# A GNN block kernel on one core: its opening in another order

## The chip, the cores and the metric

One NeuronCore of a Trainium2 chip. The metric is device time in microseconds, the median of several executions. The engines are TensorE (PE), VectorE (DVE), ScalarE (ACT) and GpSimd (POOL); SyncE (SP) only issues DMAs here. All engines run their own instruction streams and meet through semaphores.

## The reference, cut to what matters

Four residual layers on x of 384 x 1024, each of the form x = x + layer(relu(layernorm(x))). Only the first one's start is touched:

```python
h = jnp.maximum(_layernorm(x, axis=-1), 0.0)
q = h @ wq.T + bq
k = h @ wk.T + bk
v = h @ wv.T + bv
q2 = (q @ wiq.T + biq) ...
mask = full((N, N), -inf); mask[src, dst] = softplus(edge_type_weights)[edge_type_5 - 1]
scores = einsum(q2, k2) * scale + mask
```

Then come an output projection, a relational GNN layer (8 relations, counts of edges by type edge_type_8), a SAGE layer and a sparse linear layer, all on the same 6144 edges.

## The kernel before, in words

x lies as three row tiles of 128 x 1024 (NT = 3), a matrix of 1024 x 1024 as eight column tiles (KT = 8). Every fp32 operand is split into a high part of type fp32r and a low part (value minus high part), and a product is three matmuls, high x high, high x low, low x high. For the first five projections PE works through column tiles: `column_tile` (L464 to L477) is 24 matmuls of 128 x 384, eight blocks k times three. Column tile j writes PSUM bank j % 2, so `eight_tiles` (L500) has PE wait before each tile until the tile two before it has been evacuated (the semaphore out_lo): ACT writes the high part (L1005), DVE the low part (L1400).

The order of everything is written out by hand, engine by engine, and nothing reorders it. The opening, which is what the change touches, runs like this.

- **SP** (L278 to L280) issues the three row tiles of x, then from L332 the weights: each column tile of wq comes in four pieces of 128 KB into one of four raw buffers. Ahead of the fifth tile it waits for the edge rows, stores them to DRAM (L341), waits for that store and reads them back broadcast (L285).
- **ACT** issues the four edge lists and the edge type weights (L903, L906). Then per row tile: `norm_std` (L910) takes the root of the variance, `norm_relu_0` (L930 to L934) writes relu(x * rstd + shift) to h0, tiles 0 and 1 in one instruction and tile 2 in two halves (`START`). `start_high` (L937 to L942) evacuates the transposed tile from PSUM as the high part of acts. `tile_high` (L946 to L955) rounds a transposed weight tile to its high part. After the second weight tile come two activations with table loads (L993, L995) for the softplus, and the copy of the transposed biases (L998).
- **DVE** takes the statistics of each row tile (L1262, L1266), `norm_shift` (L1273 to L1277) the reciprocal and the shift, then edge keys (L1289 to L1295), three small operations on the type weights (L1298 to L1300), `turn_tile(0, 0)` (L1329 to L1333, a transpose of the first weight tile in 32 x 32 blocks), the four `start_low` (L1351 to L1357, the low parts of acts, each behind its `start_high`), with the copy of the transposed edges between the first and the second, and `turn_tile(0, 1)`. Then low part of tile 1, `turn_tile(0, 2)`, the softplus remainder behind ACT's logarithm, three mask blocks, and the loop of L1393, whose first pass turns tile 3, makes the low part of tile 2, takes two edge comparisons (`meet`, L1302 to L1316) and only then evacuates column tile 0.
- **PE** transposes each normalised row tile (L488), with the edge rows (L426) between tiles 1 and 2, then the biases (L493), which wait for six small DMAs issued by POOL, and then begins the column tiles. The first one waits at k = 0 until three `start_low` are done, at k = 4 until all four (`turned_at`).
- **POOL** makes constants, issues the six bias DMAs (L1789), makes the low part of the first weight tile (L1794), and then, behind the copy of the edges, three subtractions (L1799).

## Time and profile before

| | |
|---|---|
| median of 3 runs | 928.07 us (927.96 to 932.13) |
| the profiled execution | 927.87 us, its span 926.1 us |
| PE busy | 906.8 us, 98% of the span |
| DVE, POOL, ACT busy | 611.5, 492.3, 359.2 us |
| data moved | 128.60 MB, mean 139 GB/s |

The span is the time from the first instruction to the last one as the profiler has it; the execution around it is 1.8 us longer. A row of a timeline gives start, duration, engine, line, operation, output <- inputs. In brackets is the idle time of the engine before it and what ended it. Line numbers are those of the kernel before.

### The profile page before, as it was taken

Reading aid. Unit: us, or ns where it says so; the run is one execution under the profiler, and the core shown is the slowest. Engines: PE = TensorE matmul, PEld = TensorE weight load, DVE = VectorE, ACT = ScalarE, POOL = GpSimd, SP = SyncE. Lnnn points to the kernel's source line nnn. Section 1 sums busy time; section 2 is a strip of 40 time slices with the busy share of each in tenths; the row PEclk is TensorE's granted clock in tenths of the full one; section 3 lists DMA queues with packets and bytes.
Section 4 is the critical chain, followed back from the end, with each engine's and each line's share of the span. In section 5 each row is a group of like instructions: output and inputs, shape, how many; then the busy total and the mean of one; then the engine's idle time right before and its main releaser. Section 6 shows DMA issues by size and latency. Waiting matters only on the chain.

```text
span 926.1 us, 13755 instructions
## 1 busy us (share of the span) xinstructions
PE 906.8 (98%) x4787; PEld 799.0 (86%) x4787; DVE 611.5 (66%) x993; ACT 359.2 (39%) x558; POOL 492.3 (53%) x436
## 2 busy tenths in 40 slices
PE   4999999999999999999999999999999999999998
PEld 4999999998888888888888888888888878888886
DVE  6998888896996735665656565565656565434545
ACT  6433333345885343223223223232325235224422
POOL 5334446775765515757657575756686402220463
PEclk8999999999999999999999999999999999999999
DMA  8998756634336644344554444444333534323412
GB/s 207 241 277 224 229 155 151 167 85 119 53 52 204 178 155 146 92 151 114 152 152 130 153 113 150 113 148 111 97 91 137 182 98 154 114 93 91 140 42 91
DMA packets 89907, 128.60 MB, mean 139 GB/s; under 512 B 34480, under 2 KB 67456, under 8 KB 89856
## 3 DMA queue, kind: packets, MB, share of 16 engines
q1 hardware_dynamic: 72784, 123.54, 43.8%
q0 software_dynamic: 15552, 0.11, 4.0%
q10 hardware_dynamic: 1520, 4.30, 1.4%
q8 instruction: 29, 0.48, 0.2%
q14 instruction: 22, 0.18, 0.1%
HBM read 117.17 MB, written 7.59 MB: 135 GB/s over the span
## 4 chain that ended last, share of the span: by engine, by line
PE 90%; DVE 3%; ACT 2%; POOL 1%; DMA 1%; issue 1%; POOLq 0%; DVEq 0%; ACTq 0%
PE ps L682 49%; PE ps L476 17%; PE ps L756 9%; PE ps L520 4%; PE ps L645 4%; PE ps L600 2%; PE ps L543 2%; PE ps L556 2%; DMA weight_d<-weight_sum,cell 1%; PE ps L435 1%; POOL weight_d L1890 1%; PE ps L892 1%; DVE wlo_all L1388 1%; POOL mean_lo L1869 0%; PE ps L443 0%
## 5 line engine op out<-in xcount | busy, mean ns | idle before, releaser
L1388 DVE TENSOR_TENSOR wlo_all<-raw,whi_all 128x1024 fp32r<-128x1024 f32 x120 | 200.4, 1681 | 119.6 <-ACT whi_all L972 118.5
L476 PE MATMUL ps<-acts,whi_all 128*128 128x384 f32 (+1 forms) x640 | 164.1, 337 | 0.8 <-DVE acts L1400 0.6
L1869 POOL TENSOR_TENSOR mean_lo<-mean_f,mean_hi 128x384 fp32r<-128x384 f32 x76 | 88.3, 1162 | 120.4 <-ACT mean_hi L1124 120.4
L1124 ACT ACTIVATE mean_hi<-mean_f 128x384 fp32r<-128x384 f32 x76 | 39.9, 525 | 277.2 <-DVE mean_f L1562 277.2
L682 PE MATMUL ps<-whi_all,mean_hi 128*128 128x512 f32 x452 | 139.5, 390 | 0.3 <-POOL mean_lo L1869 0.3
L682 PE MATMUL ps<-wlo_all,mean_hi 128*128 128x512 f32 x452 | 139.3, 389 | 0.0
L682 PE MATMUL ps<-whi_all,mean_lo 128*128 128x512 f32 x452 | 139.3, 389 | 0.0
L972 ACT ACTIVATE whi_all<-raw 128x1024 fp32r<-128x1024 f32 x120 | 125.1, 1050 | 32.0 <-PE ps L682 28.5
L476 PEld LDWEIGHTS ps<-acts,whi_all 128*128 128x128 f32 x640 | 116.8, 190 | 1.2 <-DVE acts L1400 0.9
L1890 POOL DMA_INDIRECT weight_d<-weight_sum,cell x48 | 95.5, 1989 | 30.4 <-DMA weight_d<-weight_sum,cell 17.5
L476 PE MATMUL ps<-acts,wlo_all 128*128 128x384 f32 (+1 forms) x320 | 107.6, 336 | 0.0
L1833 POOL DMA_INDIRECT count_d<-met,cell x48 | 81.3, 1693 | 45.2 <-DMA count_d<-met,cell 32.0
L682 PEld LDWEIGHTS ps<-whi_all,mean_lo 128*128 128x128 f32 x452 | 84.9, 188 | 17.7
L682 PEld LDWEIGHTS ps<-wlo_all,mean_hi 128*128 128x128 f32 x452 | 84.9, 188 | 17.6
L682 PEld LDWEIGHTS ps<-whi_all,mean_hi 128*128 128x128 f32 x452 | 83.8, 188 | 12.6 <-issue 0.7
L1820 POOL DMA_INDIRECT mask_d<-type_val,cell x48 | 52.8, 1100 | 68.1 <-DMA mask_d<-type_val,cell 58.1
L1562 DVE TENSOR_TENSOR mean_f<-ps,inv 128x384 f32<-128x384 f32 x76 | 42.1, 554 | 60.5 <-PE ps L756 59.1
L1864 POOL TENSOR_TENSOR h_row_lo<-h,h_row_hi 128x1024 fp32r<-128x1024 f32 x9 | 24.6, 2756 | 99.1 <-ACT h_row_hi L1119 99.1
L756 PE MATMUL ps<-rel_r,h_row_lo 128*128 128x384 f32 x192 | 64.9, 338 | 0.0
L756 PE MATMUL ps<-rel_r,h_row_hi 128*128 128x384 f32 x192 | 64.9, 338 | 0.0
L1005 ACT ACTIVATE acts<-ps,bcol 128x384 f32 x40 | 23.3, 582 | 100.7 <-PE ps L476 87.9
L682 PE MATMUL ps<-whi_all,h_t_hi 128*128 128x512 f32 x192 | 60.8, 398 | 0.6 <-DVE wlo_all L1388 0.5
(211 smaller groups left out, 1705.6 us busy)
## 6 DMA issues: line engine op xcount, KB each, us to landing
raw<-in_L_gnn_weight SPq DMA_DIRECT2D x64, 512.0 KB
rows_b<-rows_d SPq DMA_DIRECT2D x24, 384.0 KB, 4.8
raw<-in_L_gnn_w_gate SPq DMA_DIRECT2D x16, 512.0 KB
raw<-in_L_gnn_W_self SPq DMA_DIRECT2D x16, 512.0 KB
raw<-in_L_gnn_W_neigh SPq DMA_DIRECT2D x16, 512.0 KB
count_d<-total_r SPq DMA_DIRECT2D x8, 576.0 KB
rel_r<-count_d SPq DMA_DIRECT2D x8, 576.0 KB, 4.5
raw<-in_L_gnn_wq SPq DMA_DIRECT2D x32, 128.0 KB
```

Source lines behind the costliest of these rows:

```text
L476: mm = pe.matmul(ps[:, j % 2, 0:N], stationary[j % RING][:, k, :], acts[:, a, moving, k, :], start=i == 0, stop=i == 3 * KT - 1)
L520: mm = pe.matmul(ps[:, V_BANK[n % 4], 0:V_COLS].rearrange("p (j o) -> p j o", j=2), acts[:, 3, a, k, P * nt:P * nt + P], weight[:, slots, ...
L682: mm = pe.matmul(ps[:, 2 * nt + f, :], stationary[a][:, k, P * nt:P * nt + P], weight[slot][:, HALF * f:HALF * f + HALF], start=first and ...
L756: mm = pe.matmul(ps[:, 7 - k % 2, 0:N], h_row[a][:, s, P * k:P * k + P], edges[:, s, :], start=i == 0, stop=i == 2 * NT - 1)
L972: act.activation(whi_row[slot], raw[slot][:, :], ACT.Copy).then_inc(S["w_hi"], 1)
L1124: act.activation(mean_of(q, k, 0)[:, 0, :], sums_of(q, k), ACT.Copy).then_inc(S["mean_hi"], 1)
L1388: dve.tensor_tensor(wlo_row[slot], raw[slot][:, :], whi_row[slot].bitcast(F32), ALU.subtract)\
L1562: dve.tensor_tensor(sums_of(q, k), ps[:, 7 - k % 2, 0:N], inv[:, :], ALU.mult)\
L1820: pool.indirect_dma_start(mask_d, bass.IndirectOffsetOnAxis(ap=cell[:, 0, c:c + 1], axis=0), type_val[:, c:c + 1], None).then_inc(mask_sca ...
L1833: pool.indirect_dma_start(count_d, bass.IndirectOffsetOnAxis(ap=cell[:, 1, c:c + 1], axis=0), met[:, 1, c:c + 1], None, compute_op=ALU.add)\
L1869: pool.tensor_tensor(mean_of(q, k, 1)[:, 0, :], sums_of(q, k), mean_of(q, k, 0)[:, 0, :].bitcast(F32), ALU.subtract).then_inc(S["mean_lo"], 1)
L1890: pool.indirect_dma_start(weight_d, bass.IndirectOffsetOnAxis(ap=cell[:, 2, c:c + 1], axis=0), weight_sum[:, c:c + 1], None, compute_op=AL ...
```

## The change

It reorders the opening. The first row tile of x comes in two DMAs of half its columns, and DVE takes the statistics of each half as it lands. `norm_shift` of a tile now stands between the two halves of the next tile's statistics. Row tile 2 is normalised by DVE (`start_norm`, without the relu) rather than by ACT, and the relu is applied when ACT and DVE evacuate the transposed tile. The keys of the edges are made early, types and relation keys (`edge_types`) behind the normalisation of tile 2. PE turns the edge rows behind all three tiles, into PSUM bank 2, and the biases behind the first column tile. DVE copies the turned edges and does the three small operations on the type weights behind the fourth `start_low`, just ahead of `turn_tile(0, 1)`.

```diff
--- before.py
+++ after.py
@@ -164,7 +164,7 @@
         ps = ctx.enter_context(nc.psum_tensor("ps", [P, 8, 512], F32))
 
 
-        names = """x_in edges_in etw_in bcol_in brow_in out_stored
+        names = """x_in ends_in edges_in etw_in bcol_in brow_in out_stored
             rows_stored mask_based tables_zeroed weights_zeroed mask_in weight_in
             ident_made order_made spare_made zeros_made ones_made mask_base_made
             key_made edge_rows edges_turned edge_cols edges_moved met_made rows_free
@@ -189,6 +189,7 @@
         weights_added = [sem(f"weights_added{q}") for q in range(GROUP)]
         rel_in = [sem(f"rel_in{i}") for i in range(2)]
         x_part = [sem(f"x_part{nt}") for nt in range(NT)]
+        x_half = sem("x_half")
         v_staged = [sem(f"v_staged_{s}") for s in ("even", "odd")]
 
 
@@ -276,7 +277,9 @@
         @block.sync
         def _(sp_):
             x_rows = x.rearrange("(t p) d -> p t d", p=P)
-            for nt in range(NT):
+            sp_.dma_start(xres[:, 0, 0:HALF], x_rows[:, 0, 0:HALF]).then_inc(x_half, 16)
+            sp_.dma_start(xres[:, 0, HALF:D], x_rows[:, 0, HALF:D]).then_inc(x_part[0], 16)
+            for nt in range(1, NT):
                 sp_.dma_start(xres[:, nt, :], x_rows[:, nt, :]).then_inc(x_part[nt], 16)
 
             def key_rows(s):
@@ -423,7 +426,7 @@
             def turn_edges():
                 pe.wait_ge(S["edge_rows"], 1)
                 for f in range(4):
-                    mm = pe.transpose(ps[:, 0, EC * f:EC * f + EC], e_row[:, f, :], ident[0:EC, 0:EC])
+                    mm = pe.transpose(ps[:, 2, P + EC * f:P + EC * f + EC], e_row[:, f, :], ident[0:EC, 0:EC])
                 mm.then_inc(S["edges_turned"], 1)
 
             def turn_two(y, source, f):
@@ -481,17 +484,18 @@
 
             pe.wait_ge(S["ident_made"], 2)
             for n, (nt, k0, k1) in enumerate(START):
-                if n == 2:
-                    turn_edges()
                 pe.wait_ge(S["h_ready"], n + 1)
                 for k in range(k0, k1):
                     mm = pe.transpose(ps[:, 2 + 2 * nt + k // 4, P * (k % 4):P * (k % 4) + P],
                                       h0[:, nt, P * k:P * k + P], ident[:, :])
                 mm.then_inc(S["start_turned"], 1)
-            pe.wait_ge(S["bcol_in"], 16 * 6)
             pe.wait_ge(S["start_lo"], 1)
-            pe.transpose(ps[:, 2, 0:6 * KT], b_in[:, :], ident[0:6 * KT, 0:6 * KT]).then_inc(S["bcol_made"], 1)
-            pe.wait_ge(S["edge_cols"], 1)
+            turn_edges()
+
+            def turn_biases():
+                pe.wait_ge(S["bcol_in"], 16 * 6)
+                pe.wait_ge(S["edge_cols"], 1)
+                pe.transpose(ps[:, 2, 0:6 * KT], b_in[:, :], ident[0:6 * KT, 0:6 * KT]).then_inc(S["bcol_made"], 1)
 
             def turned_at(k):
 
@@ -567,7 +571,10 @@
                 turn_probs(0, 0)
                 turn_probs(0, 1)
 
-            eight_tiles(0, 0, ready=turned_at)
+            pe.wait_ge(S["out_lo"], O_CREDIT - 1)
+            column_tile(0, 0, 0, turned_at)
+            turn_biases()
+            eight_tiles(0, 0, first=1)
             with pe.Fori(1, 3) as g:
                 eight_tiles(g, 0)
             with pe.Fori(3, 5) as g:
@@ -900,7 +907,8 @@
         @block.scalar
         def _(act):
             for f, field in enumerate((src, dst, et8, et5)):
-                act.dma_start(e_in[:, f, :], field.rearrange("(c p) -> c p", p=P)).then_inc(S["edges_in"], 16)
+                act.dma_start(e_in[:, f, :], field.rearrange("(c p) -> c p", p=P))\
+                   .then_inc(S["ends_in" if f < 2 else "edges_in"], 16)
             act.wait_ge(S["ones_made"], 1)
             act.activation(std[:, 0, :], epsc[:, :], ACT.Sqrt).then_inc(S["ones_made"], 1)
             act.dma_start(etw_b[:, :], etw.partition_broadcast(P)).then_inc(S["etw_in"], 16)
@@ -938,8 +946,8 @@
 
                 nt, k0, k1 = START[n]
                 act.wait_ge(S["start_turned"], n + 1)
-                act.activation(acts[:, 0, 0, k0:k1, P * nt:P * nt + P], start_block(nt, k0, k1), ACT.Copy)\
-                   .then_inc(S["start_hi"], 1)
+                act.activation(acts[:, 0, 0, k0:k1, P * nt:P * nt + P], start_block(nt, k0, k1),
+                               ACT.Copy if nt < NT - 1 else ACT.Relu).then_inc(S["start_hi"], 1)
 
             HALVES = [slice(0, HALF), slice(HALF, D)]
 
@@ -980,10 +988,8 @@
             norm_relu_0(*START[0])
             norm_std(0, 1)
             norm_relu_0(*START[1])
+            norm_std(0, 2)
             start_high(0)
-            norm_std(0, 2)
-            norm_relu_0(*START[2])
-            norm_relu_0(*START[3])
             tile_high(0, 0)
             start_high(1)
             start_high(2)
@@ -1276,28 +1282,44 @@
                 dve.tensor_scalar(shift[:, nt, :], mv[:, nt, 0:1], rstd[:, nt, :], -1.0, ALU.mult, ALU.mult)\
                    .then_inc(S["shift_ready"], 1)
 
-            def start_stats(nt):
-
-                dve.wait_ge(x_part[nt], 16)
-                norm_stats(0, nt)
-
-            for nt in range(NT):
-                start_stats(nt)
-                if nt < NT - 1:
-                    norm_shift(0, nt)
-            dve.wait_ge(S["edges_in"], 16 * 4)
-            dve.scalar_tensor_tensor(e_row[:, KEY, :], e_in[:, 0, :], float(N), e_in[:, 1, :], ALU.mult, ALU.add)\
-               .then_inc(S["key_made"], 1)
-            dve.scalar_tensor_tensor(e_row[:, KEY_T, :], e_in[:, 1, :], float(N), e_in[:, 0, :], ALU.mult, ALU.add)
-            norm_shift(0, NT - 1)
-            dve.tensor_copy(e_row[:, TYPE, :], e_in[:, 3, :])
-            dve.wait_ge(S["key_made"], 1)
-            dve.scalar_tensor_tensor(e_row[:, REL_KEY, :], e_in[:, 2, :], float(N * N), e_row[:, KEY, :],
-                                     ALU.mult, ALU.add).then_inc(S["edge_rows"], 1)
-            dve.wait_ge(S["etw_in"], 16)
-            link(dve.tensor_scalar(sp[:, 0, :], etw_b[:, :], 0.0, None, ALU.max))
-            link(dve.tensor_scalar(sp[:, 1, :], etw_b[:, :], -1.0, None, ALU.mult))
-            dve.tensor_tensor(sp[:, 2, :], etw_b[:, :], sp[:, 1, :], ALU.max).then_inc(S["sp_max"], 1)
+            def edge_keys():
+
+                dve.wait_ge(S["ends_in"], 16 * 2)
+                dve.scalar_tensor_tensor(e_row[:, KEY, :], e_in[:, 0, :], float(N), e_in[:, 1, :], ALU.mult, ALU.add)\
+                   .then_inc(S["key_made"], 1)
+                dve.scalar_tensor_tensor(e_row[:, KEY_T, :], e_in[:, 1, :], float(N), e_in[:, 0, :], ALU.mult, ALU.add)
+
+            def edge_types():
+
+                dve.wait_ge(S["edges_in"], 16 * 2)
+                dve.tensor_copy(e_row[:, TYPE, :], e_in[:, 3, :])
+                dve.wait_ge(S["key_made"], 1)
+                dve.scalar_tensor_tensor(e_row[:, REL_KEY, :], e_in[:, 2, :], float(N * N), e_row[:, KEY, :],
+                                         ALU.mult, ALU.add).then_inc(S["edge_rows"], 1)
+
+            def start_norm(nt, k0, k1):
+
+                dve.wait_ge(S["shift_ready"], nt + 1)
+                dve.tensor_scalar(h0[:, nt, :].rearrange("p (f b i) -> p b f i", f=KT, b=4)[:, :, k0:k1],
+                                  xres[:, nt, :].rearrange("p (b f i) -> p b f i", f=KT, b=4)[:, :, k0:k1],
+                                  rstd[:, nt, :], shift[:, nt, :], ALU.mult, ALU.add).then_inc(S["h_ready"], 1)
+
+            dve.wait_ge(x_half, 16)
+            half_stats(0, 0)
+            dve.wait_ge(x_part[0], 16)
+            half_stats(0, 1)
+            var_of(0, 0)
+            edge_keys()
+            dve.wait_ge(x_part[1], 16)
+            half_stats(1, 0)
+            norm_shift(0, 0)
+            half_stats(1, 1)
+            var_of(0, 1)
+            dve.wait_ge(x_part[2], 16)
+            half_stats(2, 0)
+            norm_shift(0, 1)
+            half_stats(2, 1)
+            var_of(0, 2)
 
             def meet(n):
 
@@ -1352,19 +1374,31 @@
 
                 nt, k0, k1 = START[n]
                 dve.wait_ge(S["start_hi"], n + 1)
-                dve.tensor_tensor(acts[:, 0, 1, k0:k1, P * nt:P * nt + P], start_block(nt, k0, k1),
-                                  acts[:, 0, 0, k0:k1, P * nt:P * nt + P].bitcast(F32), ALU.subtract)\
-                   .then_inc(S["start_lo"], 1)
+                low, high = [acts[:, 0, a, k0:k1, P * nt:P * nt + P] for a in (1, 0)]
+                if nt < NT - 1:
+                    dve.tensor_tensor(low, start_block(nt, k0, k1), high.bitcast(F32), ALU.subtract)\
+                       .then_inc(S["start_lo"], 1)
+                else:
+                    dve.scalar_tensor_tensor(low, start_block(nt, k0, k1), 0.0, high.bitcast(F32), ALU.max,
+                                             ALU.subtract).then_inc(S["start_lo"], 1)
 
             dve.wait_ge(S["h_ready"], 1)
             turn_tile(0, 0)
+            norm_shift(0, 2)
+            start_norm(*START[2])
+            start_norm(*START[3])
+            edge_types()
             start_low(0)
-            dve.wait_ge(S["edges_turned"], 1)
-            dve.tensor_copy(e_col[:, :, :], ps[:, 0, 0:4 * EC].rearrange("p (f c) -> p f c", f=4))\
-               .then_inc(S["edge_cols"], 1)
             start_low(1)
             start_low(2)
             start_low(3)
+            dve.wait_ge(S["edges_turned"], 1)
+            dve.tensor_copy(e_col[:, :, :], ps[:, 2, P:P + 4 * EC].rearrange("p (f c) -> p f c", f=4))\
+               .then_inc(S["edge_cols"], 1)
+            dve.wait_ge(S["etw_in"], 16)
+            link(dve.tensor_scalar(sp[:, 0, :], etw_b[:, :], 0.0, None, ALU.max))
+            link(dve.tensor_scalar(sp[:, 1, :], etw_b[:, :], -1.0, None, ALU.mult))
+            dve.tensor_tensor(sp[:, 2, :], etw_b[:, :], sp[:, 1, :], ALU.max).then_inc(S["sp_max"], 1)
             dve.wait_ge(S["h_ready"], len(START))
             turn_tile(0, 1)
             dve.wait_ge(S["w_lo"], 1)
```

## Rows read from the trace of the kernel before

**Rows 1.** The page: busy time, share of the span, instructions.
```profile
PE 906.8 (98%) x4787; PEld 799.0 (86%) x4787; DVE 611.5 (66%) x993; ACT 359.2 (39%) x558; POOL 492.3 (53%) x436
```

**Rows 2.** Waits of PE from 29 us to the end, the longest one.
```profile
PE ps L585 <- DVE rinv_cols L1435: 0.8, 1, 0.8
```

**Rows 3.** Waits of PE in the first 40 us.
```profile
PE ps L493 <- DMA b_in<-in_L_gnn_biv: 3.2, 1, 3.2
PE ps L476 <- DVE acts L1400: 0.6, 1, 0.6
```

**Rows 4.** Timeline of PE, 17 to 29 us: the first matmul and the one behind the wait.
```profile
17.63 0.98 PE L476 MATMUL ps<-acts,whi_all 128*128 128x384 f32 x2 [0.21 <-DVE acts L1355]
...
28.57 0.61 PE L476 MATMUL ps<-acts,whi_all 128*128 128x384 f32 x2 [0.57 <-DVE acts L1400]
```

**Rows 5.** Timeline of DVE, 15 to 28.5 us.
```profile
15.66 2.42 DVE L1355 TENSOR_TENSOR acts<-ps,acts 128x1024 fp32r<-128x1024 f32 x3 [0.66 <-ACT acts L941]
17.99 1.24 DVE L1333 STREAM_TRANSPOSE xres<-raw 128x1024 f32<-128x1024 f32 x1
...
27.90 0.61 DVE L1400 SCALAR_TENSOR_TENSOR acts<-ps,bcol,acts 128x384 fp32r<-128x384 f32 x1
```

**Rows 6.** Timeline of DVE, 8 to 15 us.
```profile
8.72 1.28 DVE L1262 BATCH_NORM_STATS2 stats<-xres 128x6 f32<-128x512 f32 x2
...
11.23 0.16 DVE L1275 RECIPROCAL rstd<-std 128x1 f32<-128x1 f32 x1 [0.64 <-ACT std L910]
...
11.56 0.21 DVE L1293 CAST e_row<-e_in 48x128 f32<-48x128 int32 x1
...
11.89 0.15 DVE L1298 TENSOR_SCALAR sp<-etw_b 128x4 f32<-128x4 f32 x1
...
12.38 1.25 DVE L1333 STREAM_TRANSPOSE xres<-raw 128x1024 f32<-128x1024 f32 x1
13.55 1.19 DVE L1355 TENSOR_TENSOR acts<-ps,acts 128x1024 fp32r<-128x1024 f32 x1
```

**Rows 7.** DMA issues of x: smallest, median and largest time to landing.
```profile
DMA to landing us min/median/max: 3.4/4.4/6.7
```

**Rows 8.** Stretches: length; PE, PEld, DVE, ACT, POOL busy; granted clock; DMA share; GB/s.
```profile
0.00:8.40 8.40, 0.39 (x2) 0.42 (x3) 3.61 (x11) 3.31 (x5) 7.13 (x17) 1.00 0.67 224
0.00:10.80 10.80, 2.60 (x11) 2.24 (x12) 5.73 (x17) 5.27 (x7) 8.94 (x20) 1.00 0.76 232
...
14.80:21.40 6.60, 4.11 (x13) 3.98 (x14) 4.75 (x6) 3.92 (x5) 3.18 (x4) 0.50 0.61 146
21.60:28.50 6.90, 6.40 (x37) 6.08 (x36) 6.13 (x15) 4.93 (x10) 3.88 (x8) 1.00 0.97 285
```

**Rows 9.** Timeline of ACT, 6 to 14 us.
```profile
11.68 1.52 ACT L933 ACTIVATE h<-xres,shift,rstd 128x512 f32<-128x512 f32 x2 [0.48 <-DVE shift L1276]
13.66 1.06 ACT L954 ACTIVATE whi_all<-xres 128x1024 fp32r<-128x1024 f32 x1 [0.46 <-DVE xres L1333]
```

**Rows 10.** DVE operations of single shapes in the span.
```profile
L1568 DVE TENSOR_SCALAR inv<-ps 128x384 f32<-128x384 f32 x10 | 5.6, 558 | 7.5 <-PE ps L744 7.5
...
L1295 DVE SCALAR_TENSOR_TENSOR e_row<-e_in,e_row 48x128 f32<-48x128 int32 x1 | 0.3, 276 | 0.0
...
L1293 DVE CAST e_row<-e_in 48x128 f32<-48x128 int32 x1 | 0.2, 208 | 0.0
```

**Rows 11.** Timeline of POOL, 10 to 28 us.
```profile
14.80 2.36 POOL L1794 TENSOR_TENSOR wlo_all<-xres,whi_all 128x1024 fp32r<-128x1024 f32 x1 [4.59 <-ACT whi_all L954]
17.12 1.01 POOL L1799 TENSOR_TENSOR moved<-e_col,spare 128x48 f32<-128x48 f32 x3
```

**Rows 12.** Timeline around 603 us, DVE and POOL.
```profile
602.75 1.02 POOL L1869 TENSOR_TENSOR mean_lo<-mean_f,mean_hi 128x384 fp32r<-128x384 f32 x1
...
603.13 1.73 DVE L1388 TENSOR_TENSOR wlo_all<-raw,whi_all 128x1024 fp32r<-128x1024 f32 x1 [1.54 <-ACT whi_all L972]
```

**Rows 13.** Timeline of SP, 17.9 to 20 us: the edge keys are read back.
```profile
18.17 0.34 SPq L285 DMA_DIRECT2D rows_b<-rows_d  x1
```

## The prediction

> **What bounds the kernel now.** I read the page first. PE is busy for 98% of the span [rows 1], so nearly all that an edit of the other engines can give is PE's idle time. The waits of PE say where that lies: from 29 us to the end the longest wait is 0.8 us [rows 2], and none of these is touched. In the first 40 us PE waits 3.2 us for the biases and then 0.6 us for the evacuation of column tile 0 [rows 3]. The timeline of PE shows the two moments that count: the first matmul of column tile 0 starts at 17.63, and the first of column tile 2 at 28.57, after 0.57 us idle [rows 4]. Everything later follows that second moment, so the question is what sets it, and not when the first matmul starts.
>
> The timeline of DVE answers. DVE evacuates tile 0 from 27.90 to 28.51, and follows an unbroken chain from the start of `turn_tile(0, 1)` at 17.99, which I call X [rows 5]: transpose, ACT's rounding and its two table loads, the mask blocks, tile 3, the low part of tile 2, two comparisons, the evacuation. None of this is edited, and PE resumes 10.58 us behind X. X itself stands behind the fourth `start_low`. So the time moves as X moves, as long as PE is done with tile 1 by then.
>
> **The start of the chain.** I call T the start of `turn_tile(0, 0)`, 12.38 before [rows 6]. It then followed the small operations on DVE. Two things can set it now. One is DVE's own work: the third row tile of x was issued at about 1.7 and landed 6.7 us later, at 8.4 [rows 7]. One more DMA ahead of it costs SP one issue, some 0.4 us, so 8.8. Behind it come two half statistics (1.28 for a pair), a reciprocal with its shift (0.33 until the next instruction) and the variance (some 0.2) [rows 6]: T of about 10.6. The other is the first weight tile, whose landing the trace does not give. By 8.4 us 224 GB/s have moved 1.88 MB, when 1.57 MB of x and 0.1 MB of edge lists had to be there, so 0.21 MB ran ahead of what landed. With 0.52 MB for the first weight tile 2.40 MB must have moved, and at the 232 GB/s of the stretch to 10.8 us that is at 10.4 [rows 8]. With SP's extra issue it is 10.8. I take T = 10.9. The ends: 10.4, if the extra issue costs nothing, and 12.38, the only time at which the trace shows that the tile was there.
>
> **From T to X.** The steps, each as the distance from one start to the next. The transpose: 1.17 [rows 6]. `norm_shift` of tile 2, no longer hidden before T: 0.45 from the reciprocal to the first instruction that reads the shift [rows 6, 9]. Two `start_norm` of 512 elements, new on DVE. No row has this operation. From above, one element per cycle: the TENSOR_SCALAR from PSUM took 0.56 for 384 elements [rows 10], so 0.69 for 512, two of them 1.3 with the overlap of neighbours. From below, the cast with one SBUF source took 0.208 against 0.276 for the form with two at the same 128 elements, 0.53 ns per element less [rows 10]; for 512 that is 0.41, two of them 0.70. I take 0.70, since the cast is the nearest row: one source, from SBUF to SBUF. "VectorE: DVE Perf Modes" of the Trainium skill (the perf-mode tier table) gives fp32 tensor_scalar between SBUF operands twice the rate of tensor_tensor, which is the lower end too; by its 1227 ns for 2048 elements each half would take an estimated 0.42. The other edits of the stretch: `edge_types` 0.33 (11.56 to 11.89) [rows 6]; `start_low` of tile 0 1.11, its 1.19 less the overlap [rows 6]; the other three 2.33 (15.66 to 17.99) [rows 5]; the copy of the edges 0.28, by the TENSOR_SCALAR from PSUM with 192 elements fewer, less the same overlap; the three operations on the type weights 0.49 (11.89 to 12.38) [rows 6]. The sum is 1.17 + 0.45 + 0.70 + 0.33 + 1.11 + 2.33 + 0.28 + 0.49 = 6.86. Before, these steps took 5.61, with 0.66 idle for ACT in it [rows 5]; that wait goes, since ACT has no normalisation of tile 2 to do and starts rounding the weight tile at T + 1.28 as before [rows 9], well before DVE asks for the second high part at T + 4.8.
>
> One thing is added. POOL's three subtractions (1.01 in all, from 17.12) ran beside `start_low` [rows 11]; they follow the copy of the edges, so they now run beside the operations on the type weights, ahead of X. At 603 us DVE's subtraction of two SBUF operands took 1.73 beside POOL's, against some 1.2 alone, and ended 1.09 behind POOL's end [rows 12]: one of the two waits for the other. I add 0.2 (0 to 0.9).
>
> X is then 10.9 + 6.86 + 0.2 = 17.96, against 17.99: **nothing gained and nothing lost**.
>
> **What lies off the path.** The biases: their wait of 3.2 us goes, but it hid behind two others, since the third `start_low` ended at about 17.4 and POOL's low part at 17.16 [rows 5, 11]. PE now starts at T + 5.6 (three low parts done), 16.5 or so, 1.1 earlier. The granted clock was 0.50, the level of 1.2 GHz, from 14.8 to 21.4, and 1.00 (2.4 GHz) behind it, where 37 matmuls took 6.40 [rows 8], 0.17 each; at 0.50 I count twice that. If the clock rises at 21.5 again, 15 matmuls are done by then, the last 33 take 5.6, the bias transpose 0.3: PE is through with tile 1 at 27.4 and waits 1.1 us for tile 2 instead of 0.57. So the earlier start is covered by the same wait, which grows. The bias copy on ACT stands before `tile_high` of tile 2: PE turns the biases at about 23.4, when ACT has just finished the logarithm (X + 5.4), so it costs nothing; had tile 0 ended a microsecond later it would. The edge rows leave DVE at T + 2.7, 13.6 rather than 12.0; SP queues their store, the wait and the fifth weight tile behind it, but the keys were read back from 18.17 on [rows 13] and are used by the comparisons just ahead of 27.90, so there are 9 us for a transfer of 384 KB and 1.6 us of delay is hidden. Without that cover the comparisons, and with them X + 10.58, would move by what is missing. The half-row DMA gives the first statistics an earlier start, of about 0.6 us, which is lost again, since `norm_shift` of tiles 0 and 1 now waits for the next row tile's landing.
>
> **The sum.** The profiled execution took 927.87, 0.20 under the median 928.07. 927.87 - 0.03 + 0.20 = 928.04, so 928.0. What a measurement of this kernel can tell from no change is 0.5%, 4.6 us; nearly every case below is within it.
>
> **Rivals.**
> *Two engines at one port (slower).* Behind the norms DVE runs the cast and the REL_KEY operation, which reads two SBUF operands, at about T + 2.32 and T + 2.45. POOL's low part of the first weight tile starts at T + 2.42 (14.80 - 12.38) and takes 2.36 [rows 11]. By rows 12 a two-operand DVE instruction can wait to POOL's end, T + 4.78, so X comes 2.3 later. The point that decides is whether POOL is ahead of the REL_KEY operation: with norms at one element per cycle it is for certain. The time: 928.0 + 2.3 = 930.3. For it speaks that my two times differ by 0.03; against it, that DVE's instructions come back to back and POOL may find the operands taken. "SBUF — State Buffer" of the Trainium skill (the ports) calls this an exclusive lock that DVE with two SBUF inputs and GpSimd hold for a whole instruction, which agrees with the 603 us row.
> *A shorter chain (faster).* The first weight tile lands at 10.4 and POOL's subtractions cost nothing: T to X stays 6.86 and X is 17.3, or a little less if row tile 2 also lands sooner. 928.0 - 0.7 = 927.3, down to 926.9.
> *Late weight tile or slow norms without a collision.* T = 11.5, or norms of 1.3: X is 0.6 later, 928.6; both, 929.2.
> *The clock.* If the level of 1.2 GHz lasts longer, each us of it costs 0.5, the first 1.1 of that covered by PE's wait. Twice as long (6.6 more) is 3.3 - 1.1 = 2.2, 930.2; past 11 us more it would reach 0.5%.
> *The change does nothing it says* can be left aside: the order is written by hand and the engines keep it.
>
> **How the numbers follow.** Forecast (927.5 to 928.5) 0.42, the port 0.25, the shorter chain 0.20, the late one 0.08, the clock 0.05. The likeliest gives 928.0. The range goes from 927.0 to 930.4: it leaves out the far end of the shorter chain, and the late and clock cases' far ends. Faster than 0.5% is in no case, and I keep 0.02 for what I have not seen; slower by that is the clock case's end and the same, 0.03; the same 0.95.
>
> **What would show it.** Right: `turn_tile(0, 0)` at 10.7 to 11.2, `start_norm` near 0.42, the first matmul at 16.3 to 17, `turn_tile(0, 1)` within 0.4 of 18.0, PE's wait for L1400's successor grown to about 1 us. Wrong: `start_norm` at 0.69; a REL_KEY operation or cast of over 1 us beside POOL's subtraction; PE running into tile 2 without a wait, which would mean that PE and its clock set the end; or a distance from X to the matmul of tile 2 other than 10.6.

## The result and the profile after

The changed kernel takes **932.17 us** (median of 14 runs, 930.61 to 942.1), the kernel before 928.02 (14 runs): ratio 1.0053, 95% interval 1.0041 to 1.0066. That is 4.2 us slower, outside the range of the prediction. The profiled execution took 932.19, 4.32 more than the 927.87 of before. Here and below a ratio is formed over all executions of the two kernels that were measured beside each other, so it need not be the quotient of the two medians. A few executions fell into a slower state with times above 1100 us (one each of a_best and b_halves_late_edges, three of the kernel before beside the experiments); the ratios leave them out, and without them the medians of a_best and b_halves_late_edges would be 927.32 and 932.11.

The timeline of VectorE (start us, us, engine, line, operation, what ended the idle time), the counterpart of [rows 5, 6]:

```profile
9.40 0.69 DVE L1268 BATCH_NORM_STATS2 stats<-xres 128x6 f32<-128x512 f32 x1 [2.33 <-DMA xres<-in_x]
...
11.82 0.69 DVE L1268 BATCH_NORM_STATS2 stats<-xres 128x6 f32<-128x512 f32 x1 [0.56 <-DMA xres<-in_x]
...
13.65 1.25 DVE L1355 STREAM_TRANSPOSE xres<-raw 128x1024 f32<-128x1024 f32 x1
14.82 0.12 DVE L1281 RECIPROCAL rstd<-std 128x1 f32<-128x1 f32 x1
...
15.22 1.00 DVE L1303 TENSOR_SCALAR h<-xres,rstd,shift 128x512 f32<-128x512 f32 x2
16.14 0.21 DVE L1295 CAST e_row<-e_in 48x128 f32<-48x128 int32 x1
...
16.48 2.34 DVE L1379 TENSOR_TENSOR acts<-ps,acts 128x1024 fp32r<-128x1024 f32 x2
...
19.94 0.34 DVE L1396 COPY e_col<-ps 128x192 f32<-128x192 f32 x1
20.20 0.15 DVE L1399 TENSOR_SCALAR sp<-etw_b 128x4 f32<-128x4 f32 x1
...
20.79 1.25 DVE L1355 STREAM_TRANSPOSE xres<-raw 128x1024 f32<-128x1024 f32 x1
...
30.70 0.61 DVE L1434 SCALAR_TENSOR_TENSOR acts<-ps,bcol,acts 128x384 fp32r<-128x384 f32 x1
```

The chain has the order and the lengths that were foretold, but it starts late. T, the first transposition, is at 13.65 (12.38 before, 10.9 predicted), because the statistics of row tiles 1 and 2 wait until 9.40 and 11.82 for x. X, the second transposition, is at 20.79 (17.99 before). The DMA issues of those two tiles say the same (the row of [rows 7] had 3.4/4.4/6.7 for all three):

```profile
DMA to landing us min/median/max: 7.7/8.6/9.6
```

TensorE, first its longest wait between 14 and 40 us, then its timeline (compare [rows 3, 4]):

```profile
PE ps L479 <- DVE acts L1434: 2.3, 1, 2.3
```

```profile
28.69 0.34 PE L479 MATMUL ps<-acts,wlo_all 128*128 128x384 f32 x1
31.36 0.80 PE L479 MATMUL ps<-acts,whi_all 128*128 128x384 f32 x2 [2.34 <-DVE acts L1434]
31.96 0.52 PE L479 MATMUL ps<-acts,wlo_all 128*128 128x384 f32 x1
```

and stretches of the span (length; PE, PEld, DVE, ACT, POOL busy; granted clock; DMA share; GB/s). The first is the one that had the clock at 0.50 before [rows 8]:

```profile
14.80:21.40 6.60, 5.32 (x29) 4.79 (x28) 6.46 (x16) 3.45 (x5) 3.45 (x4) 1.00 0.54 112
...
31.00:32.00 1.00, 0.64 (x3) 0.64 (x4) 1.00 (x2) 0.00 (x0) 0.76 (x4) 0.82 0.89 148
32.00:35.00 3.00, 3.00 (x11) 3.00 (x10) 3.00 (x8) 1.06 (x1) 0.77 (x2) 0.50 1.10 243
35.00:36.00 1.00, 1.00 (x8) 1.00 (x7) 1.00 (x2) 0.00 (x0) 0.00 (x0) 0.98 0.98 224
```

Column tile 2 resumes at 31.36 (28.57 before), 10.57 behind X as before, after an idle time of 2.34 us in place of 0.57. Behind that idle time the granted clock falls to 0.50, which is 1.2 GHz, until about 35 us: matmuls start 0.32 apart instead of 0.17. So in this execution 2.8 us of the loss is X, and the other 1.5 belongs to the matmuls at the lower level. The two things are linked: from 14.8 to 21.4 us, where the clock was at 0.50 before, it is at 1.00, so TensorE gets through column tiles 0 and 1 in 9.5 us (19.56 to 29.03) instead of 10.4 and has the longer wait for tile 2. X differs from execution to execution: three other profiles with the same opening (a_fill, a_fill_fewer, a_split_fewer below) have it at 20.00, 21.68 and 22.01.

### The profile page after: what moved, and what is told of

It reads as the page before. It is cut to its first block, busy times and chain, and to the rows that moved or that the text cites. A ratio compares the mean times of both kernels' runs of the same rounds, so it can differ in the third digit from the quotient of the medians.

```text
span 930.4 us, 13756 instructions
## 1 busy us (share of the span) xinstructions
PE 907.4 (98%) x4787; PEld 799.6 (86%) x4787; DVE 615.5 (66%) x995; ACT 357.4 (38%) x556; POOL 500.1 (54%) x436
## 4 chain that ended last, share of the span: by engine, by line
PE 90%; DVE 3%; DMA 2%; ACT 2%; POOL 1%; issue 1%; SPq 0%; POOLq 0%; DVEq 0%; ACTq 0%
PE ps L689 49%; PE ps L479 17%; PE ps L763 9%; PE ps L524 4%; PE ps L652 4%; PE ps L607 2%; PE ps L547 2%; PE ps L560 2%; DMA weight_d<-weight_sum,cell 1%; DMA xres<-in_x 1%; PE ps L438 1%; POOL weight_d L1924 1%; PE ps L899 1%; DVE wlo_all L1422 1%; POOL mean_lo L1903 0%
## 5 line engine op out<-in xcount | busy, mean ns | idle before, releaser
L1903 POOL TENSOR_TENSOR mean_lo<-mean_f,mean_hi 128x384 fp32r<-128x384 f32 x76 | 90.2, 1186 | 118.5 <-ACT mean_hi L1130 118.5
L980 ACT ACTIVATE whi_all<-raw 128x1024 fp32r<-128x1024 f32 x120 | 125.1, 1050 | 32.0 <-PE ps L689 28.5
L1854 POOL DMA_INDIRECT mask_d<-type_val,cell x48 | 55.6, 1158 | 60.7 <-DMA mask_d<-type_val,cell 50.2
```

The costliest lines, as they stand in the source:

```text
L980: act.activation(whi_row[slot], raw[slot][:, :], ACT.Copy).then_inc(S["w_hi"], 1)
L1854: pool.indirect_dma_start(mask_d, bass.IndirectOffsetOnAxis(ap=cell[:, 0, c:c + 1], axis=0), type_val[:, c:c + 1], None).then_inc(mask_sca ...
L1903: pool.tensor_tensor(mean_of(q, k, 1)[:, 0, :], sums_of(q, k), mean_of(q, k, 0)[:, 0, :].bitcast(F32), ALU.subtract).then_inc(S["mean_lo"], 1)
```

## Experiments

**One number reads them all.** The profiled execution's time less its X is 909.88 for the kernel before, and what remains says whether something went wrong behind X. (Second column: start of VectorE's second transposition. The first three columns of numbers are those of one execution, which can lie at the edge of its runs: for b_halves_late_edges and a_fill it is the fastest of them, for a_whole 3.5 us above the median.)

| run | X | profiled us | less X | median us |
|---|---|---|---|---|
| before | 17.99 | 927.87 | 909.88 | 928.02 |
| changed | 20.79 | 932.19 | 911.40 | 932.17 |
| b_halves | 20.26 | 930.17 | 909.91 | 930.43 |
| b_rowhalves | 20.62 | 930.56 | 909.94 | 930.04 |
| b_split_last | 18.13 | 928.13 | 910.00 | 928.04 |
| b_halves_late_edges | 20.79 | 930.69 | 909.90 | 932.41 |
| b_halves_two_queues | 18.03 | 928.06 | 910.03 | 929.08 |
| b_small_ahead | 18.70 | 936.91 | 918.21 | 935.88 |
| a_whole | 20.58 | 933.28 | 912.70 | 929.76 |
| a_actnorm | 23.22 | 933.19 | 909.97 | 931.84 |
| a_whole_types | 18.25 | 932.41 | 914.16 | 929.42 |
| a_best | 17.49 | 927.38 | 909.89 | 927.36 |
| a_early_split | 21.03 | 931.15 | 910.12 | 930.44 |
| a_fill | 20.00 | 930.20 | 910.20 | 933.39 |
| a_types_fewer | 17.81 | 929.28 | 911.47 | 928.01 |
| a_whole_fewer | 20.52 | 930.56 | 910.04 | 930.12 |
| a_split_fewer | 22.01 | 931.86 | 909.85 | 932.00 |
| a_fill_fewer | 21.68 | 932.04 | 910.36 | 932.43 |

Thirteen of eighteen lie between 909.85 and 910.36. The five others are the lower clock at tile 2 (changed, a_types_fewer) and a second place at some 215 us (b_small_ahead, a_whole, a_whole_types), both told below. Names with b_ start from the kernel before, those with a_ from the changed one.

**b_halves** (only the column-half split; SyncE's part is shown, VectorE takes the statistics of each half as it lands) and **b_rowhalves** (two DMAs of 64 whole rows).

```diff
-            for nt in range(NT):
+            sp_.dma_start(xres[:, 0, 0:HALF], x_rows[:, 0, 0:HALF]).then_inc(x_half, 16)
+            sp_.dma_start(xres[:, 0, HALF:D], x_rows[:, 0, HALF:D]).then_inc(x_part[0], 16)
+            for nt in range(1, NT):
...
```

> The kernel before with the split alone: two DMAs for row tile 0, statistics of a half as it lands, old order otherwise. Theory 1: row tiles 1 and 2 land 3 us or more later, and the time is 929.5 to 932. Theory 2 (the new order is what costs): 928.0, row tiles landing at 5.6 to 6 and 8.4 to 8.8.

> The kernel before with row tile 0 in two DMAs of 64 rows each, so one DMA more in the queue but rows of 4 KB as before. If it is the one DMA more ahead of the others that delays them: as the column halves, 929.5 to 932. If it is the 2 KB pieces, of which there are twice as many: 927.9 to 928.5, with row tile 2 landing at 8.8 or sooner.

b_halves: 1.0024 (1.001 to 1.0038); b_rowhalves: 1.0023 (1.0012 to 1.0035). VectorE in b_halves, then in b_rowhalves:

```profile
8.78 1.29 DVE L1265 BATCH_NORM_STATS2 stats<-xres 128x6 f32<-128x512 f32 x2 [2.14 <-DMA xres<-in_x]
...
11.01 1.28 DVE L1265 BATCH_NORM_STATS2 stats<-xres 128x6 f32<-128x512 f32 x2
...
14.64 1.25 DVE L1343 STREAM_TRANSPOSE xres<-raw 128x1024 f32<-128x1024 f32 x1
...
20.26 1.23 DVE L1343 STREAM_TRANSPOSE xres<-raw 128x1024 f32<-128x1024 f32 x1
```

```profile
9.15 1.29 DVE L1264 BATCH_NORM_STATS2 stats<-xres 128x6 f32<-128x512 f32 x2 [1.08 <-DMA xres<-in_x]
...
11.88 1.29 DVE L1264 BATCH_NORM_STATS2 stats<-xres 128x6 f32<-128x512 f32 x2 [0.43 <-DMA xres<-in_x]
```

The split alone costs some 2.3 us, by moving X from 17.99 to 20.26. The size of a piece is not the reason, since the halves of whole rows do it too.

**b_split_last**: the last row tile in two halves in place of the first.

```diff
-            for nt in range(NT):
+            for nt in range(NT - 1):
                 sp_.dma_start(xres[:, nt, :], x_rows[:, nt, :]).then_inc(x_part[nt], 16)
+            for cols in (slice(0, HALF), slice(HALF, D)):
+                sp_.dma_start(xres[:, NT - 1, cols], x_rows[:, NT - 1, cols]).then_inc(x_part[NT - 1], 16)
```

> The kernel before with row tile 2 in two DMAs of half its columns, tiles 0 and 1 whole; VectorE waits for both halves. If one DMA more in the queue delays what is in flight whatever its place: row tile 2 (or the first weight tile) is late by 2 us or more and the time is 929.5 to 931. If only a DMA ahead of the others harms: row tile 1 at 5.6, row tile 2 at 8.4 to 9, 927.9 to 928.6.

0.9999 (0.9985 to 1.0014), and the statistics start at 4.36, 6.64 and 8.85, without a wait for tiles 1 and 2. Two halves at this place, with only the weights queued behind them, do no harm.

**b_halves_late_edges**: b_halves, with ScalarE's five loads issued once row tile 0 is there.

```diff
+            act.wait_ge(x_part[0], 16)
             for f, field in enumerate((src, dst, et8, et5)):
```

> The kernel before with the split in column halves and with ScalarE issuing its five loads only when row tile 0 has landed, so that nothing but x and the weights is in flight before. If the late landings come from the other queue's small transfers meeting a fourth large one: row tiles 1 and 2 land at about 5.6 and 8 again and the time is 928 to 929 (or a little more, where the edges now are late). If they come from the fourth DMA on SyncE's queue alone: they land at 8.5 and 10.7 as in the run with the split, 930 or more.

1.0039 (1.0017 to 1.0061), worse. The two whole tiles took 5.6 and 7.8 us to land, in b_halves 7.0 and 8.8, and before no tile took over 6.7 [rows 7]. The last tile is there at 10.0 us, against 11.0 in b_halves and 8.4 before, which is neither of the two cases expected; ScalarE's standard deviations and the edges came late instead. The edge loads are a part of the cause, not the whole of it.

**b_halves_two_queues** (b_halves with the second half issued by ScalarE ahead of its own loads) and **b_small_ahead** (the kernel before with one small DMA ahead of the three tiles).

```diff
-            sp_.dma_start(xres[:, 0, HALF:D], x_rows[:, 0, HALF:D]).then_inc(x_part[0], 16)
+            act.dma_start(xres[:, 0, HALF:D], x.rearrange("(t p) d -> p t d", p=P)[:, 0, HALF:D]).then_inc(x_part[0], 16)
...
+            sp_.dma_start(x_few[:, :], x_rows[:, 0, 0:4]).then_inc(x_extra, 16)
             for nt in range(NT):
```

> The kernel before with row tile 0 in two halves, the first on SP's queue as now, the second on ScalarE's queue ahead of the edges. If the delay comes from one more DMA ahead of tiles 1 and 2 in their own queue: they land at 5.6 and 8.4 us as before, time 928.0 to 928.4 (one issue on ScalarE ahead of the edges). If it comes from the halves themselves, on whatever queue: tiles 1 and 2 land at about 8.5 and 10.7 us, time 930.4.

> The kernel before with one DMA of 128 rows of 16 bytes put ahead of the three whole row tiles on SP's queue, into a buffer that nothing reads. If one more DMA ahead, however small, is what delays the tiles behind it: stats of tiles 1 and 2 at about 8.5 and 10.7 us or later, time near 930.4. If the halves matter for their bytes: every tile lands one issue later (0.4 us), time 928.0 to 928.4.

b_halves_two_queues: 1.0008 (0.9988 to 1.0029); b_small_ahead: 1.0055 (1.0034 to 1.0076). VectorE in the one and in the other:

```profile
4.26 1.29 DVE L1265 BATCH_NORM_STATS2 stats<-xres 128x6 f32<-128x512 f32 x2 [2.66 <-DMA xres<-in_x]
...
6.55 1.27 DVE L1265 BATCH_NORM_STATS2 stats<-xres 128x6 f32<-128x512 f32 x2
...
8.76 1.28 DVE L1265 BATCH_NORM_STATS2 stats<-xres 128x6 f32<-128x512 f32 x2
...
18.03 1.23 DVE L1343 STREAM_TRANSPOSE xres<-raw 128x1024 f32<-128x1024 f32 x1
```

```profile
4.92 1.29 DVE L1265 BATCH_NORM_STATS2 stats<-xres 128x6 f32<-128x512 f32 x2 [3.33 <-DMA xres<-in_x]
...
7.21 1.27 DVE L1265 BATCH_NORM_STATS2 stats<-xres 128x6 f32<-128x512 f32 x2
...
9.42 1.28 DVE L1265 BATCH_NORM_STATS2 stats<-xres 128x6 f32<-128x512 f32 x2
...
18.70 1.24 DVE L1336 STREAM_TRANSPOSE xres<-raw 128x1024 f32<-128x1024 f32 x1
```

With the halves on two queues the tiles are there as before. With a small DMA ahead the statistics start 0.7 us later (I had put 0.4 on the split). So neither "one more DMA ahead" nor "halves" is enough by itself: the delay of the last tile by 2.6 us (b_halves) to 3.5 (b_rowhalves) takes two half tiles ahead of whole tiles in one queue.

The time of b_small_ahead, 935.88, is another matter: all its ten runs lie at 931.33 or above, where 928.0 to 928.4 was expected, and the profiled one is 8.3 us too long for its X. TensorE waits 3.1 us at the second place, told below, and has the clock at 0.50 for some 7 us there; 2.5 of the 8.3 us lie behind 235 us and were not followed. Why a small DMA at the start should bring the mask late so often is open.

What the DMA engines moved between 4 and 5 us differs, first before, then changed:

```profile
DMA packets 149, 0.39 MB, mean 392 GB/s; under 512 B 20, under 2 KB 58, under 8 KB 149
```

```profile
DMA packets 86, 0.21 MB, mean 215 GB/s; under 512 B 8, under 2 KB 35, under 8 KB 86
```

The rate falls from 392 to 215 GB/s. It is 244 in b_halves and 197 in b_rowhalves, but 392, 395 and 408 in b_split_last, b_halves_two_queues and b_small_ahead, with the engines' busy share at 0.95 or more in these seven: the packets take longer. Without the edge loads (b_halves_late_edges) it is 172, at a share of 0.73.

The rate is the smaller part. By 8.4 us 1.72 MB have been moved in the changed kernel and 1.88 before, 0.16 less, which is 0.7 us at the 224 GB/s of [rows 8]; but the last row tile lands 3.4 us later. SyncE's queue, up to that landing (packets, MB, share of the 16 engines; to 8.4 us before, to 11.8 changed):

```profile
q1 hardware_dynamic: 656, 1.78, 61.8%
```

```profile
q1 hardware_dynamic: 1407, 2.34, 78.9%
```

x is 1.57 MB of it. What SyncE issues behind x is weights, so 0.77 MB of them had been moved when the last tile was there, against 0.21 before (b_halves 0.66, b_rowhalves 0.55, b_small_ahead 0.09). The tile does not only move more slowly, it is overtaken by what is queued behind it. Why two half tiles bring that about stays open.

**a_whole**: the changed kernel with row tile 0 in one DMA again.

```diff
-            sp_.dma_start(xres[:, 0, 0:HALF], x_rows[:, 0, 0:HALF]).then_inc(x_half, 16)
-            sp_.dma_start(xres[:, 0, HALF:D], x_rows[:, 0, HALF:D]).then_inc(x_part[0], 16)
-            for nt in range(1, NT):
+            for nt in range(NT):
```

> The changed kernel with its first row tile of x in one DMA again (L280 of before); DVE waits for the whole tile and the rest of the new order stays. Theory 1 (the split delays the landings of row tiles 1 and 2, which were at 9.4 and 11.8 us against 5.6 and 8.4 before, and all else follows from that): they land at about 5.6 and 8.4 again, the first weight tile is turned at about 11, X is near 18.0 and the median is 927.6 to 928.4. Theory 2 (the new order itself is slow, whatever the landings): above 930. Theory 3 (the landings are late because of something else at the start and the split is not its cause): row tile 2 still lands behind 10 us and the time stays near 932.

1.0018 (1.0002 to 1.0034), from 927.67 to 935.56. The tiles land as before and T is 11.26, as expected, but X is 20.58 and not near 18.0, because this comes in between (both engines):

```profile
13.68 2.38 POOL L1824 TENSOR_TENSOR wlo_all<-xres,whi_all 128x1024 fp32r<-128x1024 f32 x1 [3.45 <-ACT whi_all L959]
13.76 2.39 DVE L1292 CAST e_row<-e_in 48x128 f32<-48x128 int32 x1
16.07 0.27 DVE L1294 SCALAR_TENSOR_TENSOR e_row<-e_in,e_row 48x128 f32<-48x128 int32 x1
```

The cast of `edge_types` takes 2.39 us beside GpSimd's low part, 0.21 in the changed kernel where it started at 16.14 and GpSimd at 16.23. This is the rival of the two engines at one port, in its place. By "SBUF — State Buffer" of the Trainium skill (SBUF: two separate sides), the shared pair of ports goes for a whole instruction to whichever starts first, a GpSimd operation or a VectorE one that has two SBUF inputs or runs in a two-port mode. The rows agree that one of the two waits, but the recorded starts do not tell which one. GpSimd is 0.08 ahead of the cast here, and the cast waits; in a_fill, below, it is 0.07 ahead, the cast takes its usual 0.21, and GpSimd takes 2.71 instead of some 2.4:

```profile
15.29 2.71 POOL L1831 TENSOR_TENSOR wlo_all<-xres,whi_all 128x1024 fp32r<-128x1024 f32 x1 [5.04 <-ACT whi_all L965]
```

```profile
15.36 0.21 DVE L1298 CAST e_row<-e_in 48x128 f32<-48x128 int32 x1
```

In the changed kernel GpSimd is 0.05 ahead of the REL_KEY operation, which takes its 0.28, and GpSimd takes 2.57. So who wins is settled within less than a tenth of a us, and either can.

The profiled execution of a_whole also has a wait of 2.7 us at the second place, told below, which is its 912.70.

**a_actnorm**: the split kept; ScalarE normalises tile 2 as before, VectorE's two `start_norm` are out.

```diff
-            start_norm(*START[2])
-            start_norm(*START[3])
...
+            norm_relu_0(*START[2])
+            norm_relu_0(*START[3])
```

> The changed kernel, split kept, with row tile 2 normalised by ACT again (two instructions of 0.8 us ahead of its first evacuation) and DVE's two taken out. Theory 1: the chain still begins late, since row tile 2 lands near 11.8; DVE saves 0.9 us, ACT is busy 1.5 us more, so X is between 0.9 us earlier and 0.6 us later, 931.3 to 932.8. If DVE's normalisation were what made the time: 928 to 929.

1.0038 (1.0025 to 1.0052): with x late, this part of the change moves the median by 0.3 us, no more than the spread. The median lies in the range expected, X does not: it is 23.22, 2.4 later than in the changed kernel, where 0.9 earlier to 0.6 later was expected. From T to X it takes 9.05 us instead of 7.14, with VectorE waiting 2.2 and 0.6 us for ScalarE's high parts. TensorE then waits only 0.2 us for tile 2 and the clock stays at 1.00 there, so the 1.5 us of the changed kernel are not paid. That the two times come out alike is in part chance.

**a_whole_types** and **a_best**: a_whole with `edge_types` ahead of `turn_tile(0, 0)`, where GpSimd does not work yet; a_best moves `edge_keys` and the three operations on the type weights there as well (its diff is shown; a_whole_types has only the line of `edge_types`).

```diff
-            edge_keys()
...
+            edge_keys()
+            edge_types()
+            dve.wait_ge(S["etw_in"], 16)
+            link(dve.tensor_scalar(sp[:, 0, :], etw_b[:, :], 0.0, None, ALU.max))
...
             dve.wait_ge(S["h_ready"], 1)
             turn_tile(0, 0)
             norm_shift(0, 2)
             start_norm(*START[2])
             start_norm(*START[3])
-            edge_types()
...
-            dve.wait_ge(S["etw_in"], 16)
-            link(dve.tensor_scalar(sp[:, 0, :], etw_b[:, :], 0.0, None, ALU.max))
...
```

> The changed kernel with row tile 0 whole and the cast and REL_KEY operation moved ahead of the transpose of the first weight tile. In the run with the whole tile alone the cast took 2.39 us, its end 0.08 behind POOL's subtraction of 2.38 us that had started 0.08 before it. Theory 1 (VectorE waited for a port that GpSimd held for its whole instruction): the cast takes 0.21 again, X is 0.3 + 2.2 us earlier, near 18.1, and the median is 927.6 to 928.3, with little spread. Theory 2 (the new order is slower for another reason, the cast only stood where something else was late): the 2.2 us turn up at another instruction and the median stays at 929.5 to 930.

> The same, and in addition the two key operations and the three small operations on the type weights stand ahead of that transpose as well, where VectorE waits for the first weight tile. If only the work between the start of the transpose and X counts (0.49 less of it), and no port collision is left (the key operation took 1.23 us beside GpSimd when it stood early): X near 17.4 to 17.7, 927.3 to 927.7, below the kernel before. If the first weight tile or the clock sets the end: 927.9 to 928.3.

a_whole_types: 1.0014 (0.9999 to 1.003), 927.73 to 933.11. X is 18.25, near the 18.1 expected, and the cast takes 0.17, which is what a cast ahead of GpSimd's operation should do. The median of 929.42 and the spread were not expected: seven runs lie from 927.73 to 929.54, five from 930.87 to 933.11, and the profiled one (932.41) is among the upper. **The second place**: the attention stage waits for the mask. SP's reload of it, VectorE's first score maximum and TensorE's wait for it:

```profile
212.40 0.39 SPq L374 DMA_DIRECT2D mask<-mask_d  x1
```

```profile
216.60 0.56 DVE L1451 CUSTOM_DVE_ANT_0 sc_more<-ps,mask 128x384 f32<-128x384 f32 x1 [7.57 <-DMA mask<-mask_d]
```

```profile
PE ps L544 <- DVE nmax L1451: 2.8, 1, 2.8
```

```profile
217.50:220.90 3.40, 3.20 (x15) 2.77 (x16) 2.74 (x13) 2.44 (x9) 0.12 (x1) 0.51 1.07 392
```

and the kernel before at the same place:

```profile
204.27 0.39 SPq L374 DMA_DIRECT2D mask<-mask_d  x1
```

```profile
208.67 0.55 DVE L1421 CUSTOM_DVE_ANT_0 sc_more<-ps,mask 128x384 f32<-128x384 f32 x1
```

GpSimd writes the mask with 48 scatters, two in flight, each pair waiting for the landing of the one ahead. The first starts at 36.95 before and at 37.21 here, the last at 202.07 and at 210.16: the landings, not the start, spread it. Once VectorE waits 7.5 us, TensorE runs dry for 2.8, and the clock falls to 0.50 for 3.4 us behind it, 1.5 us more: 914.16 - 909.88 = 4.3. In a_whole TensorE waits nearly as long for the same maximum,

```profile
PE ps L544 <- DVE nmax L1451: 2.7, 1, 2.7
```

and the clock stays at 1.00 behind it: 912.70 - 909.88 = 2.8, the wait alone.

a_best: 0.9992 (0.9975 to 1.0009), nine of ten runs from 927.18 to 928.32:

```profile
8.33 0.69 DVE L1265 BATCH_NORM_STATS2 stats<-xres 128x6 f32<-128x512 f32 x1 [0.82 <-DMA xres<-in_x]
...
11.27 1.25 DVE L1350 STREAM_TRANSPOSE xres<-raw 128x1024 f32<-128x1024 f32 x1
...
17.49 1.24 DVE L1350 STREAM_TRANSPOSE xres<-raw 128x1024 f32<-128x1024 f32 x1
```

X is 17.49, 0.5 earlier than before, and so is the profiled time. It is the fastest of all: eight of its ten runs lie below 927.71, the lowest of the 35 runs of before beside it. The interval of the ratio, which a run of 932.64 widens, does not exclude no difference.

**a_early_split**: a_best with only the split put back.

> The version that was fastest (edge keys, edge types and the table's three operations all ahead of VectorE's first transposition, row tile 0 in one DMA) with only the split put back. Theory that the split alone costs by the late landings: stats of tile 2 at about 12 instead of 8.8 us, first transposition 13.7, second about 19.9, time 929.5 to 930 (2.3 us over 927.4). Rival, that the order around the edges is what costs and the split is hidden once the edges are done early: 927.4 to 928.

1.0033 (1.002 to 1.0046), 930.44, with X at 21.03 where 19.9 was expected. The median is 3.1 us over a_best. The order of the edges does not cover the split.

**a_types_fewer**, **a_whole_fewer**, **a_split_fewer**: a_whole_types, a_whole and the changed kernel without the 8 last scatters of the mask.

```diff
-            landed(sp_, mask_scattered, EC)
+            landed(sp_, mask_scattered, 40)
...
-                    for m in range(MASK_ALONE + c, min(MASK_ALONE + c + GROUP, EC)):
+                    for m in range(MASK_ALONE + c, min(MASK_ALONE + c + GROUP, 40)):
```

> The version with row tile 0 in one DMA and the edge types early, whose 8 last scatters of the mask are left out (40 of 48 issued, so 8 x 128 edges are missing from the mask): the mask can be read back some 20 us earlier. Theory that the spread of 927.7 to 933.1 comes from executions in which the mask lands too late for VectorE's first score maximum: all executions at 927.7 to 928.3, no wait of TensorE for nmax, clock 1.00 at 217 to 221 us. Rival, that the spread comes from the opening or from the clock by itself: same spread, median 929.4.

> The changed kernel with row tile 0 in one DMA, and the same 8 scatters left out. It keeps the cast beside GpSimd's subtraction (2.39 us instead of 0.2). Theory: what the collision costs is left alone, 2.4 us later evacuation of the first column tile, so about 930 with a small spread. Rival, that the collision is hidden and all of the 929.8 was the late mask: 927.9.

> The changed kernel whose 8 last scatters of the mask are left out (8 x 128 edges are missing from the mask), so that the mask cannot come late. Theory that its median of 932.2 is the late opening (2.8 us) and the clock at column tile 2 (1.5 us), and only its upper executions (933.3 to 942) are the mask: median 931 to 932, highest execution below 933.5, TensorE still waits 2.3 us at tile 2. Rival, that the mask also carries the median: 930 to 930.5.

a_types_fewer: 927.57 to 929.62, ratio 0.9999 (0.9987 to 1.0011); the executions from 930.9 to 933.1 are gone, so they most likely were the mask, as the one with a profile was. Its profiled one, 929.28, waits 2.4 us at tile 2 and has the clock at 0.50 behind it: 911.47, as the changed kernel's 911.40. a_whole_fewer: 1.0014 (1.0004 to 1.0023), three runs at 927.96 to 928.58 and eight at 929.65 to 930.56, with a cast of 2.40 us in the profiled one (X 20.52, against 17.81 without the cast there): the port costs some 2 us where it strikes, and it seems not to strike in every execution (none of the three low runs has a profile, so this is not shown). a_split_fewer: 932.0, against 932.17 with the whole mask, highest 933.86 instead of 942.1: the mask is most likely the upper tail of the changed kernel, and not its median. Its VectorE shows the other face of the split:

```profile
10.86 0.69 DVE L1268 BATCH_NORM_STATS2 stats<-xres 128x6 f32<-128x512 f32 x1 [0.92 <-DMA xres<-in_x]
...
15.32 2.46 DVE L1297 SCALAR_TENSOR_TENSOR e_row<-e_in,e_row 48x128 f32<-48x128 int32 x1
...
22.01 1.25 DVE L1355 STREAM_TRANSPOSE xres<-raw 128x1024 f32<-128x1024 f32 x1
```

Here x landed 1 us sooner than in the changed kernel's profile, and the port took more than that back: 2.46 us for the REL_KEY operation.

**a_fill** and **a_fill_fewer**: the changed kernel, and a_split_fewer, with 12 matmuls that nobody reads where TensorE waits at tile 2.

```diff
+                    if first and j == 2:
+                        for i in range(12):
+                            pe.matmul(ps[:, 3, 0:N], acts[:, a, 0, i % KT, 0:P], acts[:, a, 0, i % KT, :],
+                                      start=True, stop=True)
                     pe.wait_ge(S["out_lo"], g * KT + (j - 1 + O_CREDIT))
```

> The changed kernel with 12 matmuls of 384 columns added on TensorE between column tiles 1 and 2, into a bank of PSUM that nothing reads; they fill about 2.1 us (12 x 0.174) of the 2.34 us that TensorE waits there for VectorE. Clock theory: tile 2 still resumes at about 31.4 us, but the granted clock stays 1.00 from 31 to 36 us and the run ends 1.5 us earlier than the changed kernel, about 930.7. Rival, that the loss is all in the late arrival and the lower clock costs nothing because something else bounds that stretch: 932.2, unchanged.

> The changed kernel with the 12 filler matmuls between column tiles 1 and 2 and the 8 last mask scatters left out. Theory that the clock costs what the profile says (24 matmuls of 384 columns at half rate, 1.5 us): median 1 to 1.5 us under a_split_fewer, no granted clock of 0.50 from 31 to 36 us. Rival, that the lower clock is covered: the same median as a_split_fewer. If the 931.5 to 939.9 of the filler version was not the mask, its spread stays wide here.

TensorE and the clock in a_fill:

```profile
28.93 2.24 PE L510 MATMUL ps<-acts 128*128 128x384 f32 x12
31.01 0.51 PE L479 MATMUL ps<-acts,whi_all 128*128 128x384 f32 x2
31.36 0.33 PE L479 MATMUL ps<-acts,wlo_all 128*128 128x384 f32 x1
```

```profile
31.00:36.00 5.00, 5.00 (x30) 5.00 (x30) 4.99 (x9) 1.57 (x3) 0.94 (x3) 1.00 1.02 221
```

The profiled execution fits the clock theory: idle time filled, clock 1.00, 910.20 instead of 911.40, after 0.4 us lost because the filler ran on past the evacuation (31.01 is X + 11.01). It is no clean test of it. The clock had been at 0.50 from some 18.2 to 21.7 us there, so tile 1 ended later, and without the filler TensorE would have waited only some 1.5 us, not 2.3. The medians do not bear the theory out: 933.39 (930.2 to 939.87; 1.0069, 1.0046 to 1.0092) and 932.43 against 932.0 for a_split_fewer. Neither profile of the pair without the 8 scatters has the clock at 0.50 at tile 2 (a_split_fewer waits 0.9 us there). So the 1.5 us are read from the profile of the changed kernel and of a_types_fewer, in both with the matmuls at half their rate. They seem a cost of some executions only, and that a filler wins them back is not shown.

## Why the prediction was wrong

- **The step that failed**: "One more DMA ahead of it costs SP one issue, some 0.4 us, so 8.8." The tile landed at 11.8, its statistics began at 11.82, and T was 13.65, not 10.9. A small DMA ahead costs 0.7; two halves in one queue cost 3 us, since the whole tile behind them is slower and 0.77 MB of weights, instead of 0.21, are moved before it is complete. I priced the issue and left the transfers alone.
- **A second term was put at nothing**: "So the earlier start is covered by the same wait, which grows." It grew to 2.3 us, not 1.1, because the low clock of the start, which I had carried over ("If the clock rises at 21.5 again"), was not there. Behind that wait the clock fell, 1.5 us in the profiled execution. With 2.75 us of T and 0.08 from T to X this makes the 4.3 us by which the profiled execution is longer than forecast.
- **The bounds of T** (10.4 to 12.38) were taken from rows of before, all with whole tiles ahead; I took the upper end for safe, and no rival had a late x. With the tile whole T was 11.00 to 11.44 in five profiles, in two of them behind a wait of 0.4 us for the weight tile, so the 10.9 was 0.1 to 0.5 low.
- **From T to X** held: 7.14 measured for 6.86 + 0.2, with errors of up to 0.2 that partly cancel. The `start_norm` pair takes 0.92 from its start to the next (545 ns each in the mean), not 0.70, between the two ends; `norm_shift` 0.40 for 0.45, `edge_types` 0.34 for 0.33, the `start_low` 3.46 for 3.44, the copy 0.26 for 0.28, the type weights 0.59 for 0.49 + 0.2. ("T + 4.8" for the second high part should read T + 3.8 by the same steps; nothing waited for it.)
- **From X to tile 2** held, 10.57 for 10.58. That everything later follows this moment held also, but for the clock and the mask. None of the signs of being wrong that I had listed came, since all of them lie behind T.
- **The biases** cost nothing, as said. TensorE's first matmul came at 19.56, not 16.5, with X late.
- **The clock** rival had the wrong place: in the profile the lower level did not last longer at the start, it was absent there, and it came at tile 2, behind 2.3 us idle, for 1.5 us.
- **The port** rival (930.3, a chance of 0.25) is what the order does with a whole tile: a_whole_fewer has 930.12, with some 2 us more in 8 of 11 runs than in the other three. The late x does not move it away, since both engines follow T: GpSimd starts at T + 2.58 in the changed kernel and at T + 2.57 in a_split_fewer, the REL_KEY operation at T + 2.63 in both. In the first GpSimd gives way (2.57 us), in the second VectorE does (2.46 us).
- **The first statistics** did start sooner, at 3.47 for 4.2, and it was lost, as said. The chance of 0.95 for no difference, with 0.03 for slower by 0.5%, was far too sure when the ratio came out at 1.0053: I let each step be off by tenths, and the one part that touches a shared queue was off by 3 us.
